# Attention: the block's own keys rotated before they are scaled, one power for keys and queries of a block, rows normalised on VectorE

## What is computed

```python
q = (x @ wq).reshape(B, L, 16, 128); k = (x @ wk).reshape(B, L, 4, 128); v = (x @ wv).reshape(B, L, 4, 128)
q = rms_norm(q, q_norm_w); k = rms_norm(k, k_norm_w)
k_ctx = rms_norm((ctx @ wk_ctx).reshape(B, T, 4, 128), k_norm_w)   # context keys: not rotated
q = q * cos + rotate_half(q) * sin
k = k * cos + rotate_half(k) * sin
scores = q k_full^T / sqrt(128) + mask;  out = softmax(scores) v_full @ wo
```

## Time and profile before

| | before |
|---|---|
| median of 3 runs | 1593.38 us (1588.73 to 1594.07) |
| profiled execution, its own time | 1596.49 us, span 1594.9 us |
| TensorE busy (matmul) | 1429.1 us, 90% |
| VectorE busy | 1161.5 us, 73% |
| ScalarE busy | 973.8 us, 61% |
| GpSimd busy | 782.6 us, 49% |
| mean granted TensorE clock | 0.958 of full speed |

### The profile page before, as it was taken

The page is one execution under the profiler, slowest core; times in us unless marked ns, Lnnn a source line. Parts: engine busy times, 40 slices in busy tenths (PEclk is TensorE's granted clock), DMA queues, the critical chain, the costliest instruction groups (busy, mean ns, idle before and its releaser), DMA issues. The chain is left out here.

```text
span 1594.9 us, 24846 instructions
## 1 busy us (share of the span) xinstructions
PE 1429.1 (90%) x7777; PEld 1063.4 (67%) x7820; DVE 1161.5 (73%) x2820; ACT 973.8 (61%) x2678; POOL 782.6 (49%) x888
## 2 busy tenths in 40 slices
PE   6788989989989899899887789999998799999988
PEld 5666767767767677677675556666665566666653
DVE  5666786867777768677778765556566888888774
ACT  6565665666756656567565664555564666667655
POOL 5556576666665756666656500000003455555444
PEclk9789998989999999999999899999999999999999
DMA  7334554545545546465487998888884401111000
GB/s 277 73 75 118 121 132 107 120 109 131 127 115 119 137 102 133 97 141 128 99 222 182 260 321 271 263 260 262 269 257 146 151 21 47 54 54 41 27 14 27
DMA packets 321890, 223.74 MB, mean 140 GB/s; under 512 B 276960, under 2 KB 277088, under 8 KB 320352
## 3 DMA queue, kind: packets, MB, share of 16 engines
q1 hardware_dynamic: 321760, 222.16, 51.2%
HBM read 113.05 MB, written 41.94 MB: 97 GB/s over the span
## 5 line engine op out<-in xcount | busy, mean ns | idle before, releaser
L871 DVE SCALAR_TENSOR_TENSOR planes<-E,small,planes 128x384 f16<-128x384 f32 (+1 forms) x256 | 226.6, 904 | 23.3 <-POOL planes L1078 21.0
L1078 POOL TENSOR_SCALAR planes<-E,small 128x384 f16<-128x384 f32 (+1 forms) x256 | 160.1, 638 | 155.6 <-DVE small L892 146.3
L420 PE MATMUL bank<-wq,xT 128*128 128x512 f32 x768 | 202.4, 413 | 10.9 <-ACT wq L562 9.5
L669 ACT ACTIVATE E<-E,small 128x384 f32<-128x384 f32 (+1 forms) x256 | 170.4, 666 | 67.9 <-DVE small L884 64.6
L1301 PE MATMUL bank<-wq,ot 128*128 128x512 f32 x768 | 188.6, 405 | 11.0 <-DMA ot<-ot_scratch 6.3
L884 DVE CUSTOM_DVE_ANT_0 E<-quad,mask,small 128x384 f32<-128x384 f32 (+1 forms) x256 | 169.9, 673 | 28.9 <-PE quad L450 28.8
L1301 PEld LDWEIGHTS bank<-wq,ot 128*128 128x128 f32 x768 | 148.5, 194 | 45.2 <-DMA ot<-ot_scratch 6.8
L420 PEld LDWEIGHTS bank<-wq,xT 128*128 128x128 f32 x768 | 145.7, 197 | 41.4 <-issue 9.7
L478 PE MATMUL bank<-PT,vv 128*128 128x512 f16 x672 | 161.7, 381 | 0.0
L1597 POOL TENSOR_TENSOR cl<-cl,fixed 128x1 f32<-128x1 f32 x16 | 8.8, 550 | 280.1 <-DVE cl L1481 280.1
L1065 POOL TENSOR_TENSOR t<-t 128x512 f32<-128x512 f32 x64 | 83.5, 1304 | 105.0 <-DVE t L858 105.0
(11 more groups left out here) (312 smaller groups left out, 3426.7 us busy)
## 6 DMA issues: line engine op xcount, KB each, us to landing
ot_scratch<-OT SPq DMA_DIRECT2D x64, 512.0 KB, 2.8
ot<-ot_scratch SPq DMA_DIRECT2D x64, 512.0 KB, 5.2
wkv_f<-in_w SPq DMA_DIRECT2D x12, 512.0 KB, 4.5
wkc_f<-in_w SPq DMA_DIRECT2D x12, 512.0 KB, 5.7
wkv_f<-in_wg SPq DMA_DIRECT2D x11, 512.0 KB, 7.2
wkv_f<-in_wd SPq DMA_DIRECT2D x11, 512.0 KB, 6.7
wkv_f<-in_wu SPq DMA_DIRECT2D x10, 512.0 KB, 7.0
stg<-in_ctxT SPq DMA_DIRECT2D x16, 256.0 KB, 3.0
```

The costliest lines, as they stand in the source:

```text
L420: ins = pe.matmul(bQ[:], xT[p][:, k, qt * 128:qt * 128 + 128], wq[j][:, g, k, :], start=(part == 0 and k == 0), stop=(part == 2 and k == 3))
L669: act.activation(p, p, ACT.Exp, bias=nm[:, i % 2, h:h + 1], scale=-1.0, accum_out=sm[:, i % 2, h:h + 1]).then_inc(f["s_exp"], 1)
L871: dve.scalar_tensor_tensor(plane(i, 1, h), E[:, h, 0:width(i)], ri[:, i % 2, h:h + 1], plane(i, 0, h), ALU.mult, ALU.subtract).then_inc(f[ ...
L1078: pool.tensor_scalar(plane(i, 0, h), E[:, h, 0:width(i)], ri[:, i % 2, h:h + 1], 1.0, ALU.mult, ALU.mult).then_inc(f["p_n"], 1)
```

## The change

Three things. (1) Own keys: ScalarE copies them raw (`act_k_raw`), GpSimd rotates the raw copy, and ScalarE scales the rotated result in place (`act_k_scale`) at the end of the odd block. Context keys are scaled as before, but in even blocks behind the third exponential. (2) One `act_ve` and one power (`pool_rs`) of up to 6 columns for each e: 2 columns of unit e and 4 of block e-1; there are two buffers for the result. (3) The rows of the next batch are normalised on VectorE (`dve_ln_b`), and both of their turns move behind the second head's scores. The order in the steps moves with it. The core of the diff:

```diff
+    def normed(e):
+        return slice(0 if e < NBLK else 2, 6 if e else 2)
 
     def pe_k_turn(u):
-        bg, own = unit(u)
-        if own:
-            pe.wait_ge(f["k_rope"], bg + 1)
-        else:
-            pe.wait_ge(f["k_n"], u + 1)
+        own = unit(u)[1]
+        pe.wait_ge(f["k_n"], u + 1)
 
     def pe_step(i):
-        if i % 2 == 0 and i:
+        late = i % 2 == 0 and i
+        if late:
             pe_kv(i + 2, 0)
             pe_k_turn(i + 1)
-            if turn:
-                pe_x_turn(2 * (i // 8) + 2)
             pe_kv(i + 2, 1)
         pe_s(i, 0)
         pe_s(i, 1)
-        if turn:
-            pe_x_turn(2 * (i // 8) + 3)
...
+        if turn:
+            pe_x_turn(2 * (i // 8) + 2)
+            pe_x_turn(2 * (i // 8) + 3)
         pe_s(i, 2)
 
+    def act_k_raw(u):
+        if u >= NU or not unit(u)[1]:
+            return
+        act.wait_ge(f["kv_mm"], u + 1)
+        after(act, f["kt_mm"], u)
+        act.copy(kn, kv4(u)[:, 0]).then_inc(f["k_raw"], 1)
+
+    def act_k_scale(u):
+        if u >= NU or not unit(u)[1]:
+            return
+        act.wait_ge(f["k_rope"], u // 2 + 1)
+        act.wait_ge(f["n_rs"], u + 1)
+        for t in range(2):
+            ins = act.activation(ka[:, t], ka[:, t], ACT.Copy, scale=rs6[:, u % 2, t:t + 1])
+        ins.then_inc(f["k_n"], 1)
+
+    def act_ve(e):
+        if e > NBLK:
+            return
+        c = normed(e)
+        after(act, f["k_sq"], min(e + 1, NU))
+        after(act, f["q_sq"], e)
+        after(act, f["n_rs"], e)
+        act.activation(ve6[:, c], ss[:, c], ACT.Copy, bias=128e-6).then_inc(f["n_ve"], 1)
 
     def act_step(i):
         act_o(i - 2)
         if i % 2 == 0 and i:
+            act_q_sq(i + 1)
             act_k_hi(i + 1)
-            act_q_sq(i + 1)
+            act_k_sq(i + 2)
+            act_ve(i + 2)
             act_v_hi(i + 1)
-            act_k_sq(i + 2)
...
-        if turn:
-            act_x_hi(2 * (i // 8) + 2)
         act_exp(i, 0)
         act_exp(i, 1)
+        if i % 2 or i == 0:
+            act_k_raw(i + 2)
+            act_k_sq(i + 2)
+            act_ve(i + 2)
         if turn:
+            act_x_hi(2 * (i // 8) + 2)
             act_x_hi(2 * (i // 8) + 3)
-        if i % 2 or i == 0:
-            act_k_sq(i + 2)
-        else:
-            act_k_n(i + 2)
         act_exp(i, 2)
-        if i % 2 or i == 0:
-            act_k_n(i + 2)
+        act_k_n(i + 2)
         act_exp(i, 3)
...
         act_q_hi(i + 1)
+        act_k_scale(i + 2)
 
+    def dve_ln_b(m):
+        dve.wait_ge(f["ln_rs"], m + 1)
+        dve.tensor_scalar(x, x, mv[:, 2 * t:2 * t + 1], rs[:, t:t + 1],
+                          ALU.subtract, ALU.mult).then_inc(f["ln_x"], 1)
 
     def dve_step(i):
         if i % 2 == 0 and i:
+            if turn:
+                dve_ln_b(2 * (i // 8) + 2)
             dve_o_lo(i - 2)
             dve_k_lo(i + 1)
             if turn:
-                dve_x_lo(2 * (i // 8) + 2)
+                dve_ln_b(2 * (i // 8) + 3)
+            dve_v_lo(i + 1)
             dve_ev(i, 0)
-            dve_v_lo(i + 1)
             dve_ev(i, 1)
...
-        if turn:
-            dve_x_lo(2 * (i // 8) + 3)
         dve_ev(i, 2)
+        if turn:
+            dve_x_lo(2 * (i // 8) + 2)
+            dve_x_lo(2 * (i // 8) + 3)
         dve_p_lo(i, 0)
 
+    def pool_rs(e):
+        if e > NBLK:
+            return
+        c = normed(e)
+        pool.wait_ge(f["n_ve"], e + 1)
+        pool.tensor_tensor(rs6[:, e % 2, c], ve6[:, c], half[:, c], ALU.pow).then_inc(f["n_rs"], 1)
 
     def pool_step(i):
         pool_q_add(i + 1)
-        if i:
-            pool_q_rs(i + 1)
-        if i % 2 == 0 and i:
-            pool_k_rs(i + 2)
         pool_norm(i, 0)
         pool_norm(i, 1)
-        if i % 2 or i == 0:
-            pool_k_rs(i + 2)
-        if i % 2:
-            pool_k_rope(i + 2)
+        pool_k_rope(i + 2)
+        pool_rs(i + 2)
+        pool_k_add(i + 2)
         if scaled(i):
             pool_scale(i)
         pool_norm(i, 2)
         pool_norm(i, 3)
-        if i % 2:
-            pool_k_add(i + 2)
...
         if i % 8 == 5 and i + 3 < NBLK:
-            pool_ln(2 * (i // 8) + 2)
-            pool_ln(2 * (i // 8) + 3)
+            pool_ln_rs(2 * (i // 8) + 2)
+            pool_ln_rs(2 * (i // 8) + 3)
```

More of the change, by code:

```diff
@@ L504, in pe_step @@
         pe_s(i, 1)
-        if turn:
-            pe_x_turn(2 * (i // 8) + 3)
         if i == 0:
             pe_q(1, 2)
-        if i % 2 or i == 0:
+        if not late:
             pe_kv(i + 2, 0)
             pe_kv(i + 2, 1)
+        if turn:
+            pe_x_turn(2 * (i // 8) + 2)
+            pe_x_turn(2 * (i // 8) + 3)
         pe_s(i, 2)
@@ L577, in act_x_hi, with act_k_sq @@
         act.copy(xT[0][:, :, t * 128:t * 128 + 128], xb4(m)).then_inc(f["xt_hi"], 1)
-    def act_k_sq(u, queries=None):
+    def act_k_sq(u):
         if u >= NU:
@@ L583, in act_k_sq @@
         act.wait_ge(f["kv_mm"], u + 1)
[L584 to L586 removed]
+        after(act, f["q_sq"], u)
+        after(act, f["n_ve"], u)
         for t in range(2):
[L588 removed]
+            ins = act.activation(junk[:, t, :], kv4(u)[:, 0, t], ACT.Square, accum_out=ss[:, t:t + 1])
         ins.then_inc(f["k_sq"], 1)
[L590 to L591 removed]
+    def act_k_raw(u):
[20 more added lines that the diff above has]
+        act.activation(ve6[:, c], ss[:, c], ACT.Copy, bias=128e-6).then_inc(f["n_ve"], 1)
     def act_k_hi(u):
@@ L616, in act_v_hi, with act_q_sq @@
                        scale=sig[:, bg // 4 % 2, bg % 4:bg % 4 + 1]).then_inc(f["v_hi"], 1)
-    def act_q_sq(i, keys=None):
+    def act_q_sq(i):
         if i >= NBLK:
@@ L621, in act_q_sq @@
         act.wait_ge(f["q_rope"], i + 1)
-        act.wait_ge(f["k_sq"], keys or i + 1)
-        after(act, f["q_rs"], i)
+        act.wait_ge(f["k_sq"], i + 1)
+        act.wait_ge(f["n_ve"], i + 1)
         for h in range(4):
-            ins = act.activation(junk[:, h, :], q4[:, h], ACT.Square, accum_out=qss[:, h:h + 1])
+            ins = act.activation(junk[:, h, :], q4[:, h], ACT.Square, accum_out=ss[:, 2 + h:3 + h])
         ins.then_inc(f["q_sq"], 1)
-        act.wait_ge(f["q_sq"], i + 1)
-        act.activation(qve, qss, ACT.Copy, bias=128e-6).then_inc(f["q_ve"], 1)
     def act_q_hi(i):
@@ L637, in act_k_n @@
     def act_k_n(u):
-        if u >= NU:
+        if u >= NU or unit(u)[1]:
             return
-        act.wait_ge(f["k_rs"], u + 1)
+        act.wait_ge(f["n_rs"], u + 1)
         after(act, f["kt_mm"], u)
         for t in range(2):
-            ins = act.activation(kn[:, t], kv4(u)[:, 0, t], ACT.Copy, scale=krs[:, t:t + 1])
+            ins = act.activation(kn[:, t], kv4(u)[:, 0, t], ACT.Copy, scale=rs6[:, u % 2, t:t + 1])
         ins.then_inc(f["k_n"], 1)
@@ L766, in act_program @@
         act_k_sq(0)
+        act_ve(0)
+        act_k_raw(0)
         act_w_hi(3)
-        act_k_n(0)
         act_w_hi(4)
@@ L882, in dve_ev @@
         if h == 0:
-            dve.wait_ge(f["q_rs"], i + 1)
+            dve.wait_ge(f["n_rs"], i + 2)
         dve.tensor_tensor_reduce(E[:, h, 0:n], bank_s(i, h)[:, 0:n], mask[:, 512 - n:512],
-                                 scale=cq[:, i % 2, h:h + 1], scalar=3.0e38, op0=ALU.add, op1=ALU.min,
+                                 scale=rs6[:, (i + 1) % 2, 2 + h:3 + h], scalar=3.0e38, op0=ALU.add, op1=ALU.min,
                                  accum_out=nm[:, i % 2, h:h + 1]).then_inc(f["s_ev"], 1)
@@ L996, in dve_program @@
         dve_ln_a(1)
+        dve_ln_b(0)
+        dve_ln_b(1)
         dve_w(0)
@@ L1031, in pool_c_lo, with pool_ln_rs @@
                            ALU.subtract).then_inc(f["c_lo"], 1)
-    def pool_ln(m):
-        t, x = m % 2, x_slot(m)
+    def pool_ln_rs(m):
+        t = m % 2
         pool.wait_ge(f["ln_var"], m + 1)
-        g_.did(pool.tensor_tensor(rs[:, t:t + 1], ve[:, t:t + 1], half[:, 0:1], ALU.pow))
-        g_.settle()
-        pool.tensor_scalar(x, x, mv[:, 2 * t:2 * t + 1], rs[:, t:t + 1], ALU.subtract, ALU.mult).then_inc(f["ln_x"], 1)
-    def pool_k_rs(u):
-        if u >= NU:
+        pool.tensor_tensor(rs[:, t:t + 1], ve[:, t:t + 1], half[:, 0:1], ALU.pow).then_inc(f["ln_rs"], 1)
+    def pool_rs(e):
+        if e > NBLK:
             return
-        pool.wait_ge(f["k_ve"], u + 1)
-        pool.tensor_tensor(krs[:, 0:2], kve[:, 0:2], half[:, 0:2], ALU.pow).then_inc(f["k_rs"], 1)
+        c = normed(e)
+        pool.wait_ge(f["n_ve"], e + 1)
+        pool.tensor_tensor(rs6[:, e % 2, c], ve6[:, c], half[:, c], ALU.pow).then_inc(f["n_rs"], 1)
     def pool_k_rope(u):
-        if u >= NU:
+        if u >= NU or not unit(u)[1]:
             return
-        pool.wait_ge(f["k_n"], u + 1)
+        pool.wait_ge(f["k_raw"], u // 2 + 1)
         after(pool, f["k_rope"], u // 2)
@@ L1052, in pool_k_rope @@
         pool.tensor_tensor(kb[:, :, 64:128], kn[:, :, 0:64], tab[:, 3, :, 64:128], ALU.mult)
+        g_.did(pool.tensor_tensor(ka, kn, tab[:, 2, :, :], ALU.mult))
     def pool_k_add(u):
```

(5 more changed lines are left out.)

43 lines of the change are left out of this document (16 added, 27 removed).

## The result

The changed kernel takes 1653.37 us (median of 4 runs, 1651.09 to 1655.21); the kernel before took 1593.24 beside it. The ratio is 1.0369, 95% interval 1.035 to 1.0388: 60 us slower. The forecast was 1655 in a range of 1600 to 1690.

What follows compares the result with a forecast made beforehand. A chain through GpSimd, VectorE and ScalarE, not TensorE's wait for rotated keys, was taken as the bound. Ordinary pairs' 73 us less 11 at changes of batch gave +62, hence 1655 us, range 1600 to 1690.

Steps and rivals of the forecast that it cites:

- second chain: Loop through GpSimd's probabilities, VectorE's low parts and query rotation, scores and exponentials, claimed to set the pair's length, bypassing TensorE's wait.
- first term: Odd block: GpSimd's whole rotation between heads 2 and 4 delays VectorE's low parts, less ScalarE's saved addition; +0.8 us a pair.
- second term: Query's rotation to even block's scores: ScalarE's query squares now precede the key's high part; +0.9 us a pair.
- third term: Even block, first half: value's low part now ahead of the first two score evacuations; +0.2 us, bounds 0 and 0.5.
- the clock: Rival: longer TensorE idling brings half clock, 0.5 to 1.4 us more a pair; chance 0.05 for beyond 1690 us.
- fourth term: Even block, second half: power behind heads 1 and 2, context keys' scaling ahead of the fourth exponential; +1.15 us a pair.
- The changes of batch: Pairs with a change of batch gain from normalising rows on VectorE: -1.6 us each, times 7, -11 us.
- The sum: 3.05 us a pair over 24 ordinary pairs, 73 us, less 11 at changes of batch: +62 us in total.
- faster: Rival: even blocks' scores follow the turned keys, so removing TensorE's wait gives 1537 us, or about 1565; chance 0.11.
- cancelling: Rival: gains and losses cancel to 0.4 us a pair, within 5 us of no change; chance 0.05.

Runs made afterwards that it cites:

- b_unrotated: Kernel before, own keys turned unrotated so TensorE waits only for the scaled keys, GpSimd still doing all its rotation work: 1591.84 us, ratio 0.9982.
- b_squares_first: Kernel before, one swap on ScalarE in even blocks: the query's squares ahead of the key's high part; 1621.66 us, ratio 1.0181.
- a_repaired_filled: Changed kernel with ScalarE's order and VectorE's value low part put back, even blocks' power ahead of heads 1 and 2, 8 filler matmuls before even blocks' first scores: 1597.10 us.
- a_scalar_order: Changed kernel with ScalarE's even-block order as before: key's high part, query's squares, value's high part, then next unit's squares and addition; 1629.53 us, ratio 1.0222.
- a_filled: Changed kernel with 8 filler matmuls of 512 columns on TensorE between the projection and the first scores of even blocks: 1648.50 us, ratio 1.0324.
- a_power_early: Changed kernel with the power of even blocks moved ahead of heads 1 and 2 on GpSimd: 1651.28 us, ratio 1.034.
- b_rows_again: Kernel before with only the next batch's rows normalised on VectorE and their turns moved, run again for profile and interval: 1570.61 us, ratio 0.9853.
- a_key_high_first: Changed kernel with only the key's high part put back ahead of the query's squares on ScalarE: 1644.11 us, ratio 1.0313.

## Why the prediction was right, point by point

**The chain.** That TensorE's wait for the rotated keys is worth nothing in an ordinary pair is shown by b_unrotated: no wait, same pair. That a second chain through VectorE has the length of the pair is shown by b_squares_first, which leaves the turn of the keys alone and makes each pair 1.15 longer.

**The first term, +0.8.** Counted from the odd block's first evacuation, GpSimd ends heads 1 and 2 at 4.55 (before 4.79, ScalarE's addition gone), and VectorE's low parts of heads 3 and 4 end at 11.55 (before 10.82): +0.73, and a_repaired_filled has it alone, 24.53 against 23.8. Within it two sizes were off and cancelled: the first half product behind the heads takes 0.89, not 0.46 as in the earlier trace rows, and the addition 0.73, not 1.05. The power of 6 columns takes 1.33 there, 1.34 by the slope. The raw copy, put at nothing, cost nothing: the terms below make up the whole pair without it.

**The second term, +0.9.** From the end of the queries' rotation (419.37) to the scores (421.33) it is 1.96, before 1.10: +0.86. b_squares_first, the swap alone on the old kernel, costs 1.15 with what hangs on it. But undone alone in the new kernel it gives 0.1 at full clock, since the value's high part gates the same evacuations. As a sum of separate prices this step was put too simply; together, terms two and three were 0.8 at full clock and 1.5 at half by the timelines, and a_scalar_order, which undoes both, gave back 1.0 at full clock.

**The third term, +0.2.** The changed kernel has both clocks. At full clock, TensorE and then ScalarE:

```profile
394.83 0.44 PE L449 MATMUL quad<-kT,qT 128*128 128x384 f32 x1 [3.11 <-DVE kT L849]
...
395.12 0.34 PE L450 MATMUL quad<-kT,qT 128*128 128x384 f32 x1
...
397.15 0.60 ACT L691 ACTIVATE E<-E,small 128x384 f32<-128x384 f32 x1
```

The second exponential starts 2.32 after the scores, 2.37 before: no cost. At half clock it is 424.32 - 421.33 = 2.99: +0.62. So the term's mechanism, the value's low part ahead of the evacuations, costs nothing beyond what the second term holds, and its place was taken by the clock, which I had as a rival. a_filled shows the clock's part: 27.2 to 26.5. The Trainium skill (TensorE: Matmul & The Clock Gate, HAM oscillation) describes waits that throttle the work behind them; here, where the waits are for VectorE, it is 0.7 us in six ordinary pairs (in one of them, of 28.2, on top of the cost told of below), and 2.3 at a change of batch once the early power has made TensorE's work the chain (33.2 to 30.9).

**The fourth term, +1.15.** The fourth exponential starts 4.53 after the second (before 3.36): +1.17. The power behind the heads took 1.63, between my 1.34 and 1.78. a_power_early shows the same 1.15 in pairs at full clock.

The terms of a pair at full clock add up: 0.73 + 0.81 + 1.17 = 2.7, and it takes 26.5 where it took 23.8.

**The changes of batch, -1.6.** Measured -1.5 each. TensorE, then VectorE, at one of them after:

```profile
471.06 0.44 PE L405 MATMUL bank<-fixed,kk 128*128 128x128 f32 x2 [1.02 <-ACT kk L604]
...
478.09 0.69 PE L449 MATMUL quad<-kT,qT 128*128 128x384 f32 x1 [5.16 <-DVE kT L849]
...
476.05 0.54 DVE L834 TENSOR_SCALAR stg<-stg,small 128x512 f32<-128x512 f32 x1
...
479.46 0.62 DVE L916 CUSTOM_DVE_ANT_0 E<-quad,mask,small 128x384 f32<-128x384 f32 x1 [0.23 <-PE quad L451]
```

The rows are normalised in 0.54 on VectorE, under the squares as said, and the first evacuation is 1.37 after the scores instead of 2.22. Counted from the odd block's first evacuation, the scores come 16.82 on, where they came 18.78, and the first evacuation 18.19 on, where it came 20.99: 2.8 sooner, not the 2.1 reckoned. Later in the block 1.2 of it is lost again, not 0.5; so the term is right by two errors that cancel. And TensorE idles 5.16 us ahead of them and falls to half clock all the same. The part alone is worth about 3.1 a change of batch (b_rows_again); the rest of the change eats half of it.

**The sum.** 73 - 11 = 62 was forecast for 31 pairs; 69.0 - 10.8 = 58.2 is measured over 30. That the sum comes out so near is in part luck. The mechanism as forecast gives 2.7 a pair and not 3.05, 62 us in 23 pairs. Two costs that the sum did not have add 0.7 in six pairs (the clock) and 1.05 in six (the next paragraph), 10 us together. About 5 go off again because four pairs right behind a change of batch were already longer before (24.45 to 26.09), and the rest is in single pairs at the start and end of the attention. Of the rivals, faster and cancelling fell; the one of the clock happened in part, inside the forecast's range.

**A cost that the sum did not have.** Of the seven pairs ahead of a change of batch, the six behind the first take 27.5 with any clock (28.2 where the half clock comes on top). VectorE's two low parts of such a pair, and of an ordinary one:

```profile
457.39 2.30 DVE L903 SCALAR_TENSOR_TENSOR planes<-E,small,planes 128x384 f16<-128x384 f32 x2
...
403.73 1.26 DVE L903 SCALAR_TENSOR_TENSOR planes<-E,small,planes 128x384 f16<-128x384 f32 x2
```

They take 2.30 instead of 1.26, and GpSimd's low parts of the next batch's context (`cT`, two in 3.13, from 457.72) run beside them. That this is the cause can be read from a_key_high_first, where the same pairs come in both kinds. VectorE, then GpSimd, in one ahead of a change of batch, then in the next one:

```profile
340.84 1.26 DVE L903 SCALAR_TENSOR_TENSOR planes<-E,small,planes 128x384 f16<-128x384 f32 x2
...
341.66 2.85 POOL L1067 TENSOR_TENSOR cT<-stg,cT 128x512 fp32r<-128x512 f32 x2 [0.50 <-ACT cT L570]
...
452.46 2.31 DVE L903 SCALAR_TENSOR_TENSOR planes<-E,small,planes 128x384 f16<-128x384 f32 x2
...
452.78 3.15 POOL L1067 TENSOR_TENSOR cT<-stg,cT 128x512 fp32r<-128x512 f32 x2
```

Where GpSimd begins 0.82 behind VectorE, the low parts take 1.26 and the pair 26.39; where it begins 0.32 behind, they take 2.31 and the pair 27.44. All six such pairs of that kernel fall in line, four with 2.31 and two with 1.26; in a_scalar_order five have 2.30 or 2.31 (26.5) and one 1.26 (25.64, GpSimd 1.24 behind). With the early power GpSimd always begins later, and no pair has the 2.30; so there the early power is worth 2.2 in such a pair and not 1.15 (27.5 to 25.3 with the filler). By the Trainium skill's rule on the shared SBUF interfaces (GPSIMD Engine Reference, Key points) such a collision is what should happen, since the low part has two SBUF inputs, and the trace agrees. The prediction had used this rule for the odd block only.

**What is left open.** After equal waits TensorE's first matmul runs now at half clock and now at full; no run here shows what decides it.

## What to carry to other kernels

The longest wait of the busiest engine is not the price of that wait: look at what else the waiting instruction's successor needs, and when that was ready. Here it was ready 0.11 us before, so 55.9 us of waits were worth 1 to 5 in the kernel and none in an ordinary pair, and a swap of two lines on another engine was worth 28. When the chain of a loop has been found, price every instruction that is put on it, take the gates of one instruction together and not one by one, and ask after each repair which chain comes next, at full and at half clock. Look also at what an engine off the chain now starts earlier, and beside what: here that cost as much as the clock did. A change made of several parts is best run in parts: the one of three that never touched the chain of ordinary pairs gives 23 us by itself, and with the other two the kernel takes 83 more.
